# Choosing experts for four images at a time, and splitting the query and key products from a held score buffer, in a two-layer transformer kernel

## The chip, the cores and the metric

The kernel runs on one core of a Trainium2 chip. The metric is the device time of one execution, in microseconds. Before the change it is 2116.31 us, the median of 3 runs (2114.59 to 2121.39).

## What is computed

32 images of 256 tokens, 128 features, go through two layers. Each layer is an attention with 16 heads of 8 features and a feed-forward part in which a gate chooses among 8 experts (two in layer 0, one in layer 1). Cut to what matters:

```
for layer 0 and 1:
    h = layernorm(x) * (1 + ca) + sa
    q, k, v = h @ Wq, h @ Wk, h @ Wv            # layer 0 with biases, layer 1 after one more norm
    probs = softmax(q k^T * scale [+ bias])     # 16 heads, 256 x 256
    x = x + ga * attention(probs, v)
    h = layernorm(x) * (1 + cb) + sb
    logits = h @ Wgate                          # 8 experts
    x = x + gb * sum over chosen experts of weight * expert(h)
```

## The kernel before, in words

Four stages follow one another: attention of layer 0, experts of layer 0, attention of layer 1, experts of layer 1. A barrier lies between them. The change is in the two attention stages.

**Ticks.** `run_ticks` calls `tick` once for each value of i from -LEAD to B+LAG-1. In a tick every engine works through a list written out by hand, on several images at once: `at(off)` is image i+off. The order on each engine is fixed, and an engine waits on a semaphore where an input isn't there yet. `at(0)` is the image whose raw scores are computed for the row maxima (TensorE `scores_a` into the two A buffers, VectorE `row_max`, 16 heads), `at(-1)` the image whose scores are computed again with the maxima subtracted (`scores_b`, eight chunks of two heads into the two B buffers, exponentials by ScalarE in `exps`), weighted into values (`weigh`), and so on.

**Query and key products.** For image `at(1)`, TensorE writes q and k (128 x 256 each) into M0, a PSUM bank that a dozen small products share by turns (`m0_read` is the wait for whoever read it last). ScalarE copies them out with scale and bias (`read_qk`, L701 and L703 in layer 0, L698 and L699 in layer 1). GpSimd splits each float32 value into three bfloat16 parts with four operations (`split_qk`, L602 to L605). SyncE then issues twelve DMAs (`stack_up`) that lay the parts out in `stack`, from which the scores of the next tick are computed.

**Choosing experts.** After the gate product, VectorE copies the logits (`read_logits`). For every second image, `choose_first` (and in layer 0 `choose_second`) finds the chosen experts of both images at once, `count` on TensorE turns the choices into positions, and a tick later `weigh_choices` and `place` make the row numbers (`slot_in`). GpSimd then writes the rows of each image to DRAM by indirect DMAs (`scatter`, L640: four in layer 0, two in layer 1), with one tick for each image. The rows wait in `h2` (layer 0) or `h3` (layer 1), which have HELD = 4 places.

**Order on the engines around the change.** In a tick VectorE does: maxima 0 to 5 with norms between them, `read_logits`, `residual` in layer 1 (L917), maximum 6, `choose_first` in layer 0, in layer 1 `second_stats` and `outer_norm` (L826), maximum 7, and so on to maximum 15. ScalarE does: exponential of chunk 0, small copies, chunk 1, `read_qk`, chunk 2, `max_rows`, chunk 3, `values`, and chunks 4 to 7 with copies between. TensorE does: passes a0, a1, chunk 0, a2, `weigh`, `turn_h2`, a3, chunk 1, `project_qk`, a4, `turn_heads`, a5, `gate`, chunk 2, a6, `turn_max`, `weigh`, a7, chunk 3, `project_v`, a8, and so on to a15, `turn_max`, chunk 7 and a transpose. GpSimd does: split, in layer 1 `gate_values` (L619), `modulate`, `scatter`, in layer 1 `add_experts`.

Of the kernel before, what the change touches and what calls it, by code (L numbers as in the profile page):

```python
# [12 lines left out]
P = 128  # L13
B, S, D = 32, 256, 128
NT = S // P
GROUP = 2
GT = GROUP * NT
HELD = 4
# [6 lines left out]
TOK = 256  # L25
# [108 lines left out]
def build(nc, a, out):  # L134
    with ExitStack() as ctx:
# [6 lines left out]
        def dram(name, shape, dt=F32):  # L142
# [13 lines left out]
        ident_b = sb("ident_b", [P, P], BF16)  # L156
        slope_ident = sb("slope_ident", [P, HH, P], BF16)
# [40 lines left out]
        qk = sb("qk", [P, 2, S])  # L198
# [24 lines left out]
        h3 = sb("h3", [P, HELD, NT, WX])  # L223
# [21 lines left out]
        row_dest = [sb(f"row_dest{v}", [P, NT], I32) for v in range(HELD)]  # L245
        w1s = [sb(f"w1s{u}", [P, F]) for u in range(2)]
        w2s = [sb(f"w2s{u}", [P, FC, D]) for u in range(2)]
# [3 lines left out]
        hid = [sb(f"hid{u}", [P, FC, TOK]) for u in range(2)]  # L251
        yt = [sb(f"yt{v}", [P, NT, D]) for v in range(HELD)]

        Y = [hid[0][:, 2 * u:2 * u + 2, :].rearrange("p c (t d) -> p c t d", t=NT) for u in range(2)]
# [12 lines left out]
            (ident[:, :], a["ident"]), (ident_b[:, :], a["ident_b"].bitcast(BF16)), (slope_ident[:, :, :], a["slope_ident"].bitcast(BF16)),  # L267
# [17 lines left out]
        with nc.Block() as block:  # L285
# [40 lines left out]
            def _(dve):  # L326
# [16 lines left out]
                ch.mark(dve.tensor_copy(run[:, :], region_row[:, :]))  # L343
                ch.mark(dve.tensor_tensor(qs_bias[:, :], qk_bias[:, 0:1], q_scale[:, 0:1], ALU.mult))
# [39 lines left out]
LEAD, LAG = 3, 5  # L384
# [15 lines left out]
def group_done(at, off):  # L400

    return at(off) and at(off)[2] == GROUP - 1


def attention(nc, l, g):

    (X, XR, X1, st, mv, rs, xn, hT, qk, rem, parts, stack, vals, mx, mneg, mrow, probs, heads, rsum, On, OnT, yT,
     st2, mv2, rs2, xn2, front_rows, back_rows, xb, qs_bias, h2, h3, h2T, eps_col, lg, rt, r1, sel, slot_in, token_ids, run) = (g[n] for n in (
        "X XR X1 st mv rs xn hT qk rem parts stack vals mx mneg mrow probs heads rsum On OnT yT "
# [39 lines left out]
    def scattered_before(eng, q, v):  # L449
# [5 lines left out]
    stats, xn_ready, qk_f32, x1_ready, stats2, xn2_ready, logits_read, slots_ready, pos_read = signals(  # L455
        "stats", "xn_ready", "qk_f32", "x1_ready", "stats2", "xn2_ready", "logits_read", "slots_ready", "pos_read")
# [9 lines left out]
    split, h2_ready = signals("split", "h2_ready")  # L466
# [11 lines left out]
    with nc.Block() as block:  # L478
# [111 lines left out]
        def _(pool):  # L590
# [3 lines left out]
            def split_qk(b, k, u):  # L594

                pool.wait_ge(qk_f32.handle, qk_f32.after(b))

                for half in range(2):
                    pool.wait_ge(stack_in[u][half], stack_in.of(k - 1))
                p = parts[u]  # L600
                one = ones_col[:, :, :].broadcast_to([P, 2, S])
# [30 lines left out]
            def scatter(b, k, u, q, v):  # L632
                pool.wait_ge(slots_ready.handle, slots_ready.after(k))
# [3 lines left out]
                for c in range(n_choice):  # L637
                    for t in range(NT):
                        place = slot_in[v // GROUP][:, c, u * NT + t:u * NT + t + 1]
                        pool.indirect_dma_start(gathered[l], bass.IndirectOffsetOnAxis(ap=place, axis=0),  # L640
                                                (h3 if l else h2)[:, v, t, :], None).then_inc(scat_out[v], 16)

            def tick(at):
                if at(1):
                    split_qk(*at(1))
# [4 lines left out]
                if at(-5):  # L650
                    scatter(*held(at, -5))
# [1028 lines left out]
```

## Time and profile before

| | value |
|---|---|
| median of 3 runs | 2116.31 us |
| profiled execution, its own time | 2124.9 us |
| its span, first to last instruction | 2123.1 us |
| busy share of the span | TensorE 76%, VectorE 73%, ScalarE 47%, GpSimd 41% |
| mean granted TensorE clock | 0.936 of full speed |
| attention of layer 0, about | 46 to 810 us |
| experts of layer 0, about | 814 to 1109 us |
| attention of layer 1, about | 1114 to 1908 us |
| experts of layer 1, about | 1917 to 2123 us |

The shares are averages over four stages with different limits, so the table says where to look and not what bounds. A wait is given as "[time <- engine and line]": the idle time of the engine before that row and what ended it. Busy matrix products overlap in the profile, so the busy time of TensorE can't be added up from single rows.

### The profile page before, as it was taken

What the parts mean: (1) busy time and instruction counts of PE and PEld (TensorE: products, weight loads), DVE (VectorE), ACT (ScalarE), POOL (GpSimd) and SP (SyncE); (2) the same over time, 40 slices, a digit from 0 to 9 for tenths busy, and PEclk for the clock granted to TensorE, in tenths of its full rate; (3) what the DMA queues carried; (4) which work ended last, traced back from release to release, by engine and by line L of the source; (5) the groups of instructions that cost most, each with busy time, mean ns of one, the idle gap of its engine ahead of it and who ended that gap; (6) DMA issues with size and microseconds to landing.
All of it is one profiled execution on the core that took longest, in us unless ns stands there. A gap on an engine that the chain in (4) does not pass through costs nothing. (4 is left out here: it accounts for less than half of the span.)

```text
span 2123.1 us, 43990 instructions
## 1 busy us (share of the span) xinstructions
PE 1614.7 (76%) x14050; PEld 1145.8 (54%) x14050; DVE 1540.6 (73%) x4940; ACT 1002.2 (47%) x1846; POOL 878.5 (41%) x932
## 2 busy tenths in 40 slices
PE   2388888888888863999981777777777777753996
PEld 1256555555656542999971444444444444433886
DVE  4378878888888743777753879889888988853664
ACT  0166566666665541222221455565565565541543
POOL 0123353544444432555552335454445454430544
PEclk9899999999999986999995899999999999986998
DMA  4333343343333313222226544554455554525543
GB/s 112 75 67 65 78 74 79 75 79 74 79 74 77 68 39 77 72 72 74 72 58 165 96 87 103 113 110 105 110 110 103 114 111 104 98 63 163 134 124 82
DMA packets 267468, 193.11 MB, mean 91 GB/s; under 512 B 26095, under 2 KB 257297, under 8 KB 266468
## 3 DMA queue, kind: packets, MB, share of 16 engines
q1 hardware_dynamic: 251880, 155.28, 34.7%
q0 software_dynamic: 15360, 35.03, 5.4%
q8 instruction: 114, 1.87, 0.4%
q14 instruction: 114, 0.93, 0.2%
HBM read 95.21 MB, written 53.18 MB: 70 GB/s over the span
## 5 line engine op out<-in xcount | busy, mean ns | idle before, releaser
L871 DVE TENSOR_REDUCE mx<-A 128x2 f32<-128x512 f32 x1024 | 685.6, 681 | 196.2 <-PE A L1131 170.3
L725 ACT ACTIVATE probs<-B 128x1024 f32<-128x1024 f32 x512 | 523.2, 1022 | 370.1 <-PE B L1151 188.8
L1131 PE MATMUL A<-stack 126*128 126x256 bf16 x2048 | 393.5, 281 | 139.5 <-DVE mx L871 110.9
L1151 PE MATMUL B<-stack 128*128 128x256 bf16 x2048 | 360.2, 278 | 64.6 <-DMA stack<-mrow 64.6
L1131 PEld LDWEIGHTS A<-stack 126*128 126x128 bf16 x2048 | 163.0, 99 | 302.3 <-DVE mx L871 205.6
L1169 PE MATMUL M<-probs,vals 128*32 128x256 f32 x4096 | 287.2, 397 | 27.5 <-DVE On L894 24.7
L1151 PEld LDWEIGHTS B<-stack 128*128 128x128 bf16 x2048 | 196.8, 101 | 122.4 <-DMA stack<-mrow 87.5
L626 POOL TENSOR_TENSOR h<-xn,back_rows 128x256 f32<-128x256 f32 x64 | 46.3, 724 | 496.6 <-DVE xn L826 496.6
L640 POOL DMA_INDIRECT gathered<-h,slot_in x192 | 187.1, 974 | 100.7 <-DVE slot_in L1017 52.1
L1580 PE MATMUL A<-w2s,hid 128*128 128x128 f32 x1792 | 219.6, 276 | 8.4 <-issue 8.4
L1580 PEld LDWEIGHTS A<-w2s,hid 128*128 128x128 f32 x1792 | 208.8, 192 | 12.8 <-issue 12.8
L1384 POOL DMA_INDIRECT expert_out<-yt,row_dest x144 | 142.4, 989 | 156.9 <-DVE yt L1487 122.5
L1571 PE MATMUL B<-xtT,w1s 128*128 128x256 f32 x896 | 206.3, 385 | 0.0
L1154 PE MATMUL B<-dist,slope_ident 128*128 128x128 bf16 x1024 | 183.9, 220 | 0.0
L1169 PEld LDWEIGHTS M<-probs,vals 128*32 128x32 f32 x4096 | 122.2, 112 | 111.9 <-issue 44.0
L1571 PEld LDWEIGHTS B<-xtT,w1s 128*128 128x128 f32 x896 | 169.1, 194 | 21.0
L1529 ACT ACTIVATE hid<-B 128x1024 f32<-128x1024 f32 x72 | 73.7, 1024 | 212.4 <-PE B L1571 212.4
L602 POOL TENSOR_TENSOR parts<-qk,ones_col 128x512 bf16<-128x512 f32 x64 | 66.5, 1040 | 231.8 <-ACT qk L703 142.2
L1381 POOL DMA_INDIRECT out<-yt,row_dest x80 | 78.9, 987 | 127.5 <-DVE yt L1484 109.0
L671 ACT ACTIVATE rs<-mv,eps_col 128x2 f32<-128x2 f32 x192 | 56.0, 292 | 125.8 <-DVE mv L812 72.4
L1429 DVE TENSOR_SCALAR w1s<-w 128x512 f32 x112 | 54.9, 490 | 76.4 <-PE B L1571 69.3
L1562 PE MATMUL M<-ident,xt 128*128 128x128 f32 x224 | 44.0, 279 | 81.4 <-DMA xt<-gathered 81.4
(181 smaller groups left out, 2510.9 us busy)
## 6 DMA issues: line engine op xcount, KB each, us to landing
stack<-parts SPq DMA_DIRECT2D x768, 64.0 KB
xt<-gathered SPq DMA_DIRECT2D x112, 132.0 KB, 2.2
probs<-gathered SPq DMA_DIRECT2D x40, 256.0 KB, 3.2
w<-in_w SPq DMA_DIRECT2D x4, 2048.0 KB, 10.0
back_rows<-mod_rows SPq DMA_DIRECT2D x64, 128.0 KB, 3.7
x_mid<-X SPq DMA_DIRECT2D x64, 128.0 KB, 2.4
hid<-expert_out SPq DMA_DIRECT2D x64, 128.0 KB
X<-in_x SPq DMA_DIRECT2D x32, 128.0 KB, 3.7
```

What stands on the lines that cost most here:

```text
L640: pool.indirect_dma_start(gathered[l], bass.IndirectOffsetOnAxis(ap=place, axis=0), (h3 if l else h2)[:, v, t, :], None).then_inc(scat_out ...
L725: act.activation(probs[c % 4][:, :, :, :], Bp[c % 2][:, :, :, :], ACT.Exp, scale=EXP_SCALE[l][c // 4]).then_inc(b_exp.handle, 1)
L871: dve.tensor_reduce(mx[u][:, h, :], A[h % 2][:, :, :], AX.X, ALU.max).then_inc(a_max.handle, 1)
L1131: ins = pe.matmul(A[h % 2][:, t, :], stack[u][0:n, h, 0, t * P:(t + 1) * P], stack[u][0:n, h, 1, :], start=True, stop=True)
L1151: ins = pe.matmul(Bp[c % 2][:, j, t, :], stack[u][:, h, 1, t * P:(t + 1) * P], stack[u][:, h, 0, :], start=True, stop=(l == 1))
L1154: ins = pe.matmul(Bp[c % 2][:, j, t, t * P:(t + 1) * P], slope_ident[:, h % HH, :], dist[:, :], start=False, stop=True)
L1169: ins = pe.matmul(M1[VW * j:VW * j + VW, 0:S], vals[u][:, t, first:first + VW], probs[(2 * g + j // 2) % 4][:, j % 2, t, :], start=(q == 0 ...
L1381: ins = pool.indirect_dma_start(expert_out[l], dest, yt[s % HELD][:, t, :], None, bounds_check=B * S - 1, oob_is_err=False)
L1384: ins = pool.indirect_dma_start(expert_out[l], dest, yt[s % HELD][:, t, :], None)
L1529: act.activation(hid[u][:, :, :], src, ACT.Relu).then_inc(hidden.handle, 1)
L1571: ins = pe.matmul(dst[:, f, :], w1s[u][:, f * P:(f + 1) * P], xtT[u][:, :], start=True, stop=True)
L1580: ins = pe.matmul(A[u][:, t, 0:D], hid[u][:, f, t * P:(t + 1) * P], w2s[u][:, f, :], start=(f == 0), stop=(f == FC - 1))
```

## The change

- GROUP goes from 2 to 4: experts are chosen, counted and placed once for four images, on tiles twice as wide. HELD goes from 4 to 8, and the scatter of an image comes two ticks later (`at(-7)` for `at(-5)`), so LAG goes from 5 to 7. To make room, h3 shares its memory with buffers of the expert stages, which keep four output places (OUT = 4).
- The scale of q is multiplied into wq once, in the setup, by a row loaded with one more DMA.
- `project_qk` writes into the first half of B0 and no more into M0. ScalarE makes the high part straight from there (`high_part`), VectorE subtracts it from the products (`remainder`, after maximum 6), ScalarE casts the remainder (`mid_part`, between `max_rows` and chunk 3), GpSimd makes the low part (`low_part`, which is L605 of before). B0 is held from the product to the remainder, so that chunks 1, 2 and 3 of the scores all go into B1; the eight chunks use B0, B1, B1, B1, B0, B1, B0, B1 (before: by turns).

```diff
-GROUP = 2
+GROUP = 4
-HELD = 4
+HELD = 8
+OUT = 4
...
+                ch.mark(dve.tensor_tensor(wq[:, :, :], wq[:, :, :], scale_row[:, :, :], ALU.mult))
...
-LEAD, LAG = 3, 5
+LEAD, LAG = 3, 7
+BUFFER = (0, 1, 1, 1, 0, 1, 0, 1)
+HOLD = 4
...
-                ch.link(pool.tensor_tensor(p[:, :, 0, :], qk[:, :, :], one, ALU.mult))
-                ch.link(pool.tensor_tensor(rem[:, :, :], qk[:, :, :], p[:, :, 0, :], ALU.subtract))
-                ch.link(pool.tensor_tensor(p[:, :, 1, :], rem[:, :, :], one, ALU.mult))
-                pool.tensor_tensor(p[:, :, 2, :], rem[:, :, :], p[:, :, 1, :], ALU.subtract).then_inc(split.handle, 1)
+            def low_part(b, k, u):
+                pool.wait_ge(qk_mid.handle, qk_mid.after(b))
+                pool.tensor_tensor(parts[u][:, :, 2, :], rem[:, :, :], parts[u][:, :, 1, :], ALU.subtract)\
+                    .then_inc(split.handle, 1)
...
-                if at(-5):
-                    scatter(*held(at, -5))
+                if at(-7):
+                    scatter(*held(at, -7))
...
+            def high_part(b, k, u):
                 act.wait_ge(qk_proj.handle, qk_proj.after(b))
...
+                src, dst = Bp[0][:, 0, :, :], parts[u][:, :, 0, :]
                 if l:
+                    ins = act.activation(dst, src, ACT.Copy)
                 else:
+                    ch.mark(act.activation(dst[:, 0, :], src[:, 0, :], ACT.Identity, bias=qs_bias[:, 0:1]))
+                    ins = act.activation(dst[:, 1, :], src[:, 1, :], ACT.Identity, bias=qk_bias[:, 1:2])
+                ins.then_inc(qk_high.handle, 1)
+
+            def mid_part(b, k, u):
+                act.wait_ge(qk_rem.handle, qk_rem.after(b))
+                act.activation(parts[u][:, :, 1, :], rem[:, :, :], ACT.Copy).then_inc(qk_mid.handle, 1)
...
+            def remainder(b, k, u):
+                dve.wait_ge(qk_high.handle, qk_high.after(b))
+                dve.wait_ge(split.handle, split.after(b - 1))
+                src, high = Bp[0][:, 0, :, :], parts[u][:, :, 0, :]
+                if l:
+                    ins = dve.tensor_tensor(rem[:, :, :], src, high, ALU.subtract)
+                else:
+                    ch.mark(dve.scalar_tensor_tensor(out=rem[:, 0, :], in0=src[:, 0, :], scalar=qs_bias[:, 0:1],
+                                                     in1=high[:, 0, :], op0=ALU.add, op1=ALU.subtract))
+                    ins = dve.scalar_tensor_tensor(out=rem[:, 1, :], in0=src[:, 1, :], scalar=qk_bias[:, 1:2],
+                                                   in1=high[:, 1, :], op0=ALU.add, op1=ALU.subtract)
+                ins.then_inc(qk_rem.handle, 1)
...
             def project_qk(b, k, u):
                 pe.wait_ge(h_ready.handle, h_ready.after(b))
-                pe.matmul(M0[:, 0:S], wq[:, l, :], hT[u][:, :], start=True, stop=True)
-                pe.matmul(M0[:, S:2 * S], wk[:, l, :], hT[u][:, :], start=True, stop=True).then_inc(qk_proj.handle, 1)
+                pe.wait_ge(qk_rem.handle, qk_rem.after(b - 1))
+                pe.wait_ge(b_exp.handle, b_exp.after(b - 2, 1))
+                pe.matmul(Bp[0][:, 0, 0, :], wq[:, l, :], hT[u][:, :], start=True, stop=True)
+                pe.matmul(Bp[0][:, 0, 1, :], wk[:, l, :], hT[u][:, :], start=True, stop=True).then_inc(qk_proj.handle, 1)
...
-                pe.wait_ge(b_exp.handle, b_exp.after(b, c - 1) if c >= 2 else b_exp.after(b - 1, HH + c - 1))
+                if c == HOLD:
+                    if hold is None:
+                        pe.wait_ge(b_exp.handle, b_exp.after(b, 1))
+                    else:
+                        pe.wait_ge(qk_rem.handle, qk_rem.after(hold))
+                else:
+                    last = [d for d in range(c) if BUFFER[d] == BUFFER[c]]
+                    pe.wait_ge(b_exp.handle, b_exp.after(b, last[-1] + 1) if last else b_exp.after(b - 1, HH + c - 1))
...
                 if at(1):
-                    m0_read((h2T_read, -3))
                     project_qk(*at(1))
...
                 if at(-3):
-                    m0_read((qk_f32, 1))
                     gate(*at(-3))
```

## Rows read from the trace of the kernel before

**Rows 1.** Windows: busy us (instructions) of PE, PEld, DVE, ACT, POOL; clock, DMA, GB/s.
```profile
230.00:700.00 470.00, 408.68 (x4225) 278.74 (x4226) 387.46 (x1097) 286.05 (x515) 214.49 (x220) 1.00 0.38 76
1275.00:1840.00 565.00, 435.20 (x3859) 254.82 (x3858) 497.54 (x1556) 328.88 (x637) 265.60 (x297) 0.96 0.50 108
```

**Rows 2.** Source lines L701, L698: ns min/median/max, first and last start.
```profile
L701 ACT ACTIVATE qk<-M,qs_bias,q_scale x32: 557/563/564, 64.8 to 722.0; 128x256 f32<-128x256 f32 x32
...
L698 ACT ACTIVATE qk<-M,q_scale x32: 467/473/475, 1144.7 to 1839.8; 128x256 f32<-128x256 f32 x32
```

**Rows 3.** Timeline of TensorE, layer 0: start us, us, what, [idle before].
```profile
427.53 0.44 PE L1101 MATMUL M<-ident,On 128*128 128x128 f32 x2 [0.67 <-ACT vals L711]
...
438.91 0.28 PE L1151 MATMUL B<-stack 128*128 128x256 bf16 x1 [1.02 <-DMA stack<-mrow]
...
446.89 0.27 PE L1151 MATMUL B<-stack 128*128 128x256 bf16 x1
```

**Rows 4.** Waits, 230 to 700 us: us in total, times, longest us.
```profile
PE M L1187 <- ACT qk L703: 8.9, 21, 0.6
```

**Rows 5.** Timeline of ScalarE, layer 0, chunks 1 to 3.
```profile
442.25 1.02 ACT L725 ACTIVATE probs<-B 128x1024 f32<-128x1024 f32 x1
...
445.48 1.02 ACT L725 ACTIVATE probs<-B 128x1024 f32<-128x1024 f32 x1 [1.38 <-PE B L1154]
446.40 0.36 ACT L718 ACTIVATE mrow<-M 16x256 bf16<-16x256 bf16 x1
447.75 1.02 ACT L725 ACTIVATE probs<-B 128x1024 f32<-128x1024 f32 x1 [1.00 <-PE B L1154]
```

**Rows 6.** VectorE groups, 1275 to 1840 us: busy us, mean ns, idle before.
```profile
L917 DVE TENSOR_TENSOR h<-On,xb 128x256 f32<-128x256 f32 x25 | 30.6, 1224 | 1.3
L826 DVE TENSOR_SCALAR xn<-X,mv,rs 128x128 f32<-128x128 f32 x50 | 29.7, 633 | 0.0
...
L826 DVE TENSOR_SCALAR xn<-h,mv,rs 128x128 f32<-128x128 f32 x50 | 15.0, 343 | 0.0
...
L907 DVE TENSOR_TENSOR xb<-XR,M 128x256 f32<-128x256 f32 x25 | 10.5, 421 | 0.9
```

**Rows 7.** Timeline of GpSimd, layer 1: first and last of the split's four.
```profile
1453.07 1.04 POOL L602 TENSOR_TENSOR parts<-qk,ones_col 128x512 bf16<-128x512 f32 x1 [3.70 <-ACT qk L699]
...
1456.61 1.16 POOL L605 TENSOR_TENSOR parts<-rem,parts 128x512 bf16<-128x512 f32 x1
```

**Rows 8.** Timeline of VectorE, layer 1: placing, choosing, and L917 at the end.
```profile
1466.68 0.19 DVE L1007 TENSOR_TENSOR rt<-M,run 128x32 f32<-128x32 f32 x1
...
1467.42 0.17 DVE L1017 CAST slot_in<-r 128x4 int32<-128x4 f32 x1
...
1482.83 0.16 DVE L972 TENSOR_SCALAR h<-token_ids 128x4 f32<-128x4 f32 x1
...
1484.58 0.18 DVE L979 TENSOR_TENSOR rt<-lg,r 128x32 f32<-128x32 f32 x1
...
1877.39 0.43 DVE L917 TENSOR_TENSOR h<-On,xb 128x256 f32<-128x256 f32 x1
```

**Rows 9.** Timeline of TensorE, layer 1: the transpose of the maxima.
```profile
1467.12 0.28 PE L1138 MATMUL M<-ident_b,mneg 128*16 128x128 bf16 x2 [0.63 <-DVE run L1009]
```

**Rows 10.** Timelines of VectorE and GpSimd, the ends of both attention stages.
```profile
795.18 0.36 DVE L1017 CAST slot_in<-r 128x8 int32<-128x8 f32 x1
...
808.50 0.95 POOL L640 DMA_INDIRECT gathered<-h,slot_in  x1 [0.30 <-issue]
...
1903.19 0.96 POOL L640 DMA_INDIRECT gathered<-h,slot_in  x1 [1.41 <-DVE slot_in L1017]
...
1906.98 0.96 POOL L640 DMA_INDIRECT gathered<-h,slot_in  x1 [0.30 <-issue]
```

**Rows 11.** Timeline of VectorE in the setup.
```profile
12.66 2.65 DVE L340 MEMSET h<- 128x3104 f32 x1 [0.59 <-issue]
...
16.41 0.17 DVE L343 COPY run<-region_row 128x8 f32<-128x8 f32 x1 [1.07 <-DMA wmod<-in_wmod]
```

More of the change, by code:

```diff
@@ L244, in build @@
         row_weight = [sb(f"row_weight{u}", [P, 2, NT]) for u in range(2)]
[L245 to L247 removed]
+        row_dest = [sb(f"row_dest{v}", [P, NT], I32) for v in range(OUT)]
+        w1s = [shared[:, u * F:u * F + F] for u in range(2)]
+        w2s = [shared[:, (2 + u) * F:(3 + u) * F].rearrange("p (c d) -> p c d", c=FC) for u in range(2)]
         row_end = [sb(f"row_end{u}", [P, NT, W - D]) for u in range(2)]
@@ L465, in attention @@
                                         signal("pv", 4), signal("o_T", 2))
-    split, h2_ready = signals("split", "h2_ready")
+    h2_ready, = signals("h2_ready")
+    qk_high, qk_rem, qk_mid, split = signals("qk_high", "qk_rem", "qk_mid", "split")
     if l == 1:
@@ L632, in scatter @@
             def scatter(b, k, u, q, v):
-                pool.wait_ge(slots_ready.handle, slots_ready.after(k))
+                pool.wait_ge(slots_ready.handle, slots_ready.after(b // GROUP))
                 if l:
@@ L644, in tick @@
                 if at(1):
-                    split_qk(*at(1))
+                    low_part(*at(1))
                 if l and at(1):
@@ L750, in weights @@
             def weights(b, k, u):
-                act.wait_ge(w_den.handle, w_den.after(k))
+                act.wait_ge(w_den.handle, w_den.after(b // GROUP))
                 if l:
@@ L774, in tick @@
                 chunk(1)
-                step(read_qk, 1)
+                step(high_part, 1)
                 chunk(2)
@@ L778, in tick @@
                 step(max_rows, -1, 1)
+                step(mid_part, 1)
                 chunk(3)
@@ L991, in weigh_choices @@
                 row = group_rows(v)
-                dve.wait_ge(w_exp.handle, w_exp.after(k))
+                dve.wait_ge(w_exp.handle, w_exp.after(b // GROUP))
                 if l:
@@ L1003, in place @@
             def place(b, k, u, q, v):
-                dve.wait_ge(pos.handle, pos.after(k))
+                dve.wait_ge(pos.handle, pos.after(b // GROUP))
                 ch.settle()
@@ L1061, in tick @@
                 maxima(6, 1)
+                step(remainder, 1)
                 group(0, choose_first, -3)
@@ L1218, in chunk @@
                     if at(-1):
-                        scores_b(*at(-1), c)
+                        scores_b(*at(-1), c, at(1)[0] if at(1) else None)
                 def heads_step(step, off, g):
@@ L1312, in experts @@
     xt_in = Transfers([sem(f"xt_in{u}") for u in range(2)], 1)
-    yt_out = Transfers([sem(f"yt_out{v}") for v in range(HELD)], NT, 0)
+    yt_out = Transfers([sem(f"yt_out{v}") for v in range(OUT)], NT, 0)
     extra_in = Transfers([sem(f"extra_in{u}") for u in range(2)], 1)
@@ L1389, in _ @@
                     scatter(*tile(k, n))
-            for s in range(slots - HELD, slots):
-                pool.wait_ge(yt_out[s % HELD], yt_out.of(s // HELD))
+            for s in range(slots - OUT, slots):
+                pool.wait_ge(yt_out[s % OUT], yt_out.of(s // OUT))
         @block.vector
@@ L1652, in inputs_of @@
         "qk_bias": np.stack([bqkv[0:D][stacked], bqkv[D:2 * D][stacked]], 1),
-        "q_scale": np.stack([np.where(np.arange(D) < 64, HD ** -0.5, (2.0 / HD) ** 0.5), np.full(D, D ** -0.5)], 1).astype(f),
+        "q_scale": q_scale, "scale_row": np.broadcast_to(q_scale.T[None], (P, 2, P)).copy(),
         "vo_bias": np.stack([bqkv[2 * D:][out_rows], n["L0_attn_b_out"]], 1),
```

93 lines of the change are left out of this document (42 added, 51 removed).

## The prediction, made before the changed kernel was seen

> **What bounds the kernel now.** I read the page first, for the stages, and then the windows of the steady part of each attention stage [rows 1]. In layer 0 TensorE is busy for 408.68 of 470 us (87%) and VectorE for 82%; in layer 1 it is the other way round, VectorE 497.54 of 565 us (88%), TensorE 77%. So layer 0 is near TensorE's limit and layer 1 near VectorE's, and one edit has two prices. The source lines of the copies of q, one for each image, give the length of a tick [rows 2]: (722.0 - 64.8) / 31 = 21.2 us in layer 0, (1839.8 - 1144.7) / 31 = 22.4 us in layer 1. The sum below is so much per tick times about 30, plus what happens once.
>
> The timeline of TensorE in layer 0 shows what it waits for [rows 3]: 0.67 us before a transpose for the values, 1.02 us before chunk 0 for the row of maxima to land. The list of waits adds the gate's product, which waits for q and k to be copied out of M0 [rows 4]: 8.9 / 21 = 0.42 us in a tick. In layer 1 VectorE hardly pauses before its own work (the idle column is 0.0 to 1.3 us for 25 to 50 instructions [rows 6]); it is TensorE that waits for VectorE there.
>
> **The change, part by part.**
>
> *The gate's wait, layer 0.* q and k leave M0, so these 0.42 us go. They are kept only if what follows comes earlier too. The products of a chunk start 447.75 - 446.89 = 0.86 us before its exponential [rows 3, 5]. So chunk 2's products start at 445.48 - 0.86 = 444.6, or 444.2 after the change, and B1 is free when the exponential of chunk 1 ends, 442.25 + 1.02 = 443.3: 0.9 us of slack. Chunk 3's products start at 446.89 and B1 is free at 445.48 + 1.02 = 446.5: 0.4 us of slack, and both move together. The cast `mid_part` has to fit between the exponentials of chunks 2 and 3: 447.75 - 446.50 = 1.25 us, less 0.36 us for the copy of the maxima [rows 5]. A copy of 512 elements is not in the trace; from the 1.02 us for 1024 it is between half of that, 0.51, and three quarters, 0.77. I take 0.6 us, which leaves 0.3 us, if the remainder is there. So I take 0.4 us per tick: 30 x 0.4 = 12 us. Lower end: the exponentials slip by as much, 0. Upper end: TensorE idles 61 us in 22 ticks, 2.8 us per tick [rows 1]; less 0.67, 1.02 and 0.42 some 0.7 us remain, which I put down to VectorE; half as much choosing may give back half of it, so 0.75 us per tick, 22 us.
>
> *L917 in layer 1.* It takes 1224 ns on average [rows 6], but 0.43 us at the end of the stage, where no q and k are split any more [rows 8]. In the steady part it lies under GpSimd's four operations of the split, which last 1457.77 - 1453.07 = 4.7 us [rows 7]. After the change only the fourth is left, and it can't start before the remainder, which VectorE itself does after L917. So L917 loses 0.8 us per tick whatever else moves. The Trainium skill (SBUF — State Buffer, "Who interferes with whom") says that a VectorE instruction with two inputs in SBUF contends with a GpSimd instruction that reads SBUF. By that rule the remainder, which has one input in PSUM, waits for nobody and the sum is as below; were it held as L917 is, the sum would be 0.8 us per tick, 23 us, worse.
>
> *The remainder.* It is new on VectorE. L907 is the nearest row, one input in PSUM, 256 elements, 421 ns [rows 6]. With L1007, 32 elements from PSUM in 0.19 us [rows 8], the slope is (421 - 190) / 224 = 1.03 ns per element, so 512 elements take 421 + 264 = 0.69 us in one instruction (layer 1) and 0.84 us in two (layer 0). In layer 1 this is on the path. In layer 0 TensorE is the bound and choosing is rarer, so I take nothing; if the cover is gone it costs 0.84 us in a tick, which is inside the lower end above for every second tick. Bounds in layer 1: 0.6 to 0.84 us.
>
> *`outer_norm` in layer 1* (L826, xn from X). Each of its two instructions takes 633 ns against 343 ns for the same work from h [rows 6]: 0.58 us per tick lost beside L605 and what follows it on GpSimd. These stay, and by the order on VectorE `outer_norm` comes just after remainder and maximum 7, when the cast is over and `low_part` runs. I take no change; if the stall is gone it is 0.58 x 29 = 17 us more.
>
> *Choosing for four, layer 1.* Choosing takes 1484.76 - 1482.83 = 1.93 us less some 0.6 us of a maximum between, 1.3 us; placing 1467.59 - 1466.68 = 0.9 us [rows 8], and the two small instructions for the weight 0.3 us at the same size. That is 2.5 us for two images, 1.25 us per tick. Twice the width adds 32 elements, 33 ns by the slope above, to each of 15 instructions: 3.0 us for four images, 0.75 us per tick. The gain is 0.5 us per tick. Placing also holds up the transpose of the maxima by 0.63 us [rows 9], now in every fourth tick and not in every second: 0.16 us per tick. In layer 0 the choosing lies beside TensorE, the bound: nothing beyond the above.
>
> *The gate's wait, layer 1.* Between 0 and layer 0's 0.42 us [rows 4]; TensorE is late there for VectorE's sake only, so I take 0.15 us.
>
> *Layer 1, sum per tick:* -0.80 + 0.69 - 0.50 - 0.16 - 0.15 = -0.92 us, x 29 = -27 us.
>
> *The ends.* The last group is placed as soon as the last image is chosen, as before, but now four images wait for it and not two. In layer 0 the last `slot_in` was written at 795.2 and the last scatter began at 808.50 [rows 10]. Now all 16 scatters of four images follow. Their step is (1906.98 - 1903.19) / 3 = 1.26 us, so the last begins near 795.6 + 15 x 1.26 = 814.5: +6 us. In layer 1 eight follow where four did: 4 x 1.26 = +5 us. Nothing covers this, since the barrier comes after. Together +11 us.
>
> *The starts.* For the first image the path goes through the split: 4.7 us [rows 7]. Remainder, cast and `low_part` take 0.8 + 0.6 + 1.16 us and some 0.1 us between: 2.7 us. That is -2 us in each layer, -4 us.
>
> *The setup.* The memset of h3 doubles, so it is over 2.65 us later, after 17.9 us, where the loads were awaited until 16.41 [rows 11]. With the scaling of wq (256 elements, 0.4 us): +2 us. The added DMA lies under it.
>
> *Other edits.* The expert stages have the same instructions on other addresses: nothing. The two added ticks hold only scatters, counted above. SyncE's DMAs of the parts start when `low_part` ends, about when L605 ended before: cast over at 447.4, then 1.16 us, against a tick that begins ten microseconds later.
>
> **Sum:** -12 - 27 + 11 - 4 + 2 = -30 us. Against the profiled execution, 2124.9 us with 2123.1 us of span, that is 2095. The median of the runs lies 8.6 us under that execution, so I give 2116.3 - 30 = 2086 us.
>
> **Rivals.**
>
> *A. The held buffer becomes the wait (slower).* With chunks 1, 2 and 3 through one buffer, TensorE and ScalarE have to take turns: product, exponential, product. It decides once the exponential of chunk 2 ends over 0.4 us later, against TensorE, than in rows 5. If high part, remainder and cast come so late that chunks 2 and 3 slip by 1.2 us per tick, the cost is (1.2 - 0.4) x 61 = 49 us against the -30: 2135 us. For it: the cast waits in ScalarE's ordered queue for a VectorE instruction behind maximum 6, and every later exponential is queued behind the cast. Against it: ScalarE sits idle for 1.38 and 1.00 us before these two exponentials [rows 5].
>
> *B. The steady gains are small.* VectorE's relief in layer 1 is eaten at the edge of the tick by the landing of the maxima (1.02 us, which no edit touches), and the gate's wait in layer 0 turns into a longer one for the values (0.67 us now) [rows 3]. Then 0.3 us per tick in layer 1 (-9), 0.1 in layer 0 (-3), and +9 once: 2113 us. For it: the row of the landing. Against it: VectorE's 88% in layer 1, with 0.8 us of it that surely go.
>
> *C. More stalls go than I count.* `outer_norm` is freed as well (-17 us), and layer 0 reaches its upper end (-10 us): 2059 us. It hangs on some tenths of a microsecond in the start of `low_part`, which no row shows. The Trainium skill (same page and section) says that whoever of VectorE and GpSimd starts first keeps the port for the whole instruction; no row here shows who will be first.
>
> **How the numbers follow.** A measurement of this kernel can tell about 0.3% (6 us) from no change. The forecast (2072 to 2102 us) gets 0.58, C 0.16, B 0.16, A 0.10. The time is the likeliest, 2086 us. The range leaves out A and the far half of C: 2062 to 2110 us. Faster by over 0.3%: 0.58 + 0.16 and a third of B, 0.80. Within 0.3%: half of B and a little of A, 0.11. Slower: 0.09.
>
> **What would show each step.** The gate's row in layer 0 without a wait for ScalarE, and a tick there of 20.8 us. In layer 1 L917 near 430 ns, a remainder of about 690 ns, and a tick near 21.5 us. `outer_norm` still near 630 ns; if it falls to 340, C. Sixteen and eight scatters after the last `slot_in`, and 11 us for them in all. The prediction is wrong if TensorE shows a new wait for exponentials before chunks 2 and 3 (A), or if the ticks of layer 1 stay above 22 us (B).

## The result, and the profile after

The changed kernel takes 2126.03 us (median of 10 runs, 2114.45 to 2132.24) where the kernel before took 2117.52 us beside it (10 runs): a ratio of 1.0033, 95% interval 1.0018 to 1.0049. It is slower by a third of a per cent, where I forecast 1.4% faster. Its profiled execution took 2125.89 us, 2124.1 us of it span.

First the source lines that give the ticks: starts of the copies of q and k in layer 0 (L701) and layer 1 (L699).

```profile
L701 ACT ACTIVATE parts<-B,qs_bias x32: 472/473/475, 67.4 to 710.2; 128x256 bf16<-128x256 f32 x32
```
```profile
L699 ACT ACTIVATE parts<-B x32: 591/591/598, 1140.4 to 1833.1; 128x512 bf16<-128x512 f32 x32
```

With [rows 2] they cut both executions into five stretches. I add the two halves of the change, run by themselves (below).

| us | to the first copy of q | 31 ticks, layer 0 | between the layers | 31 ticks, layer 1 | rest | span |
|---|---|---|---|---|---|---|
| before | 64.8 | 657.2 | 422.7 | 695.1 | 283.3 | 2123.1 |
| after | 67.4 | 642.8 | 430.2 | 692.7 | 291.0 | 2124.1 |
| forecast, difference | +2 | -14 | +6 | -29 | +5 | -30 |
| measured, difference | +2.6 | -14.4 | +7.5 | -2.4 | +7.7 | +1.0 |

(The splitting of q and k follows their copy, so the forecast's -2 us for each first image stand in the columns of the two layers.) Layer 0 did what was forecast. Layer 1 gave 2 us of 29, and even that flatters it: the profiled execution of before holds two ticks of 26.2 and 27.8 us in layer 1, together some 8 us above the other ticks of their kind, and lies 7 us above the median of its runs. By the medians the kernel after is 8.5 us slower, and the spans differ by 1.0. In the windows it is still VectorE that is busiest there, 487.31 us of 565 where it was 497.54 [rows 1], and the stretch is hardly shorter:

```profile
230.00:700.00 470.00, 410.09 (x4303) 284.75 (x4300) 386.25 (x1021) 305.38 (x542) 144.65 (x155) 1.00 0.41 78
1275.00:1840.00 565.00, 423.62 (x3834) 259.12 (x3838) 487.31 (x1474) 329.30 (x627) 179.50 (x218) 0.95 0.51 106
```

VectorE's groups of layer 1, answering to [rows 6]: the remainder, the addition that was L917, and `outer_norm`.

```profile
L830 DVE TENSOR_SCALAR xn<-X,mv,rs 128x128 f32<-128x128 f32 x48 | 37.3, 816 | 0.0
L876 DVE TENSOR_TENSOR rem<-B,parts 128x512 f32<-128x512 f32 x25 | 17.0, 682 | 0.0
...
L934 DVE TENSOR_TENSOR shared<-On,xb 128x256 f32<-128x256 f32 x25 | 10.7, 426 | 1.2
```

426 ns (was 1224) and 682 ns are as forecast; 816 ns (was 633) is not.

Now four ticks of layer 1 in a row, from copy to copy. Columns: window in us, its length, busy time of TensorE, its weight loads, VectorE, ScalarE, GpSimd, then granted clock, DMA share, GB/s. The first tick chooses, the second places, the other two do neither (I call them free).

```profile
1464.95:1488.44 23.49, 18.50 (x155) 10.90 (x153) 20.84 (x64) 13.32 (x27) 7.45 (x9) 0.85 0.45 100
1488.44:1510.32 21.88, 16.30 (x164) 10.29 (x162) 20.05 (x63) 13.45 (x27) 7.44 (x9) 1.00 0.55 115
1510.32:1533.38 23.06, 17.50 (x155) 10.41 (x154) 18.91 (x56) 13.08 (x26) 7.44 (x9) 0.93 0.51 111
1533.38:1557.45 24.07, 17.39 (x155) 10.40 (x154) 18.91 (x56) 13.06 (x26) 7.42 (x9) 0.93 0.53 102
```

This is the heart of the case. A free tick has 1.1 us less of VectorE's work than a tick that places, and here takes 1.2 to 2.2 us more. Over 1285 to 1812 us the six ticks that place last 21.73 us on average, the six that choose 23.58, the eleven free ones 23.18. Choosing for four makes every second tick a free one. And in eight of the eleven free ticks the granted clock is below 1.00: part of the tick was at TensorE's lower level, 1.2 GHz, and the rest at 2.4 GHz.

What is different in a free tick is how the maxima's row reaches TensorE. Timelines of SyncE's queue, GpSimd and TensorE at the end of a tick that places, then of a free one (issue of the last load, of the scatters and of the row; chunk 0):

```profile
1409.56 0.57 SPq L508 DMA_DIRECT2D gb_row<-mod_rows  x1
1412.32 0.67 SPq L542 DMA_DIRECT2D stack<-mrow  x1
```
```profile
1412.99 1.01 POOL L640 DMA_INDIRECT gathered<-shared,slot_in  x1 [3.53 <-DVE slot_in L1034]
```
```profile
1414.55 0.28 PE L1179 MATMUL B<-stack 128*128 128x256 bf16 x1 [0.85 <-DMA stack<-mrow]
```
```profile
1431.14 0.43 SPq L508 DMA_DIRECT2D gb_row<-mod_rows  x1
1433.81 0.67 SPq L542 DMA_DIRECT2D stack<-mrow  x1
```
```profile
1431.44 1.01 POOL L640 DMA_INDIRECT gathered<-shared,slot_in  x1 [0.15 <-issue]
1432.76 0.96 POOL L640 DMA_INDIRECT gathered<-shared,slot_in  x1 [0.30 <-issue]
```
```profile
1437.30 0.28 PE L1179 MATMUL B<-stack 128*128 128x256 bf16 x1 [2.59 <-DMA stack<-mrow]
```

From issue to chunk 0 it is 2.2 us in the first and 3.5 us in the second. In the first the scatters wait for `slot_in` and start behind the row; in the second they start 2.4 and 1.0 us ahead of it, and the DMA engines are full when the row is sent (share of the 16 engines and GB/s at the end of each line):

```profile
1432.00:1433.00 1.00, 1.00 (x14) 0.34 (x7) 0.93 (x6) 0.01 (x1) 0.69 (x2) 1.00 0.66 141
1433.00:1434.00 1.00, 0.65 (x5) 0.35 (x4) 1.00 (x4) 0.97 (x4) 0.72 (x1) 1.00 1.08 305
1434.00:1435.00 1.00, 0.71 (x6) 0.39 (x5) 0.93 (x6) 1.00 (x2) 0.00 (x0) 1.00 1.17 349
1435.00:1436.00 1.00, 0.00 (x0) 0.00 (x0) 1.00 (x2) 0.14 (x1) 0.00 (x0) 1.00 0.99 339
1436.00:1437.00 1.00, 0.00 (x0) 0.00 (x0) 0.07 (x1) 0.00 (x0) 0.72 (x1) 1.00 0.60 154
```

TensorE stands still through the last two of these windows. That ticks that choose keep their 2.0 us from issue to chunk 0 fits: there choosing sends the row some 2 us later, behind the burst. The Trainium skill (DMA: Bandwidth & Descriptors, "Queues, rings and completion order") says that the descriptors which SyncE issues are consumed in order on each DMA engine. From that I infer that a small row waits behind the loads issued before it; the rows above agree, without proving it. The scatters come through another queue, GpSimd's.

The kernel before shows the same once. In its tick of 27.8 us, one that chooses, the row went out as close behind two scatters as in a free tick of the kernel after:

```profile
1488.23 1.01 POOL L640 DMA_INDIRECT gathered<-h,slot_in  x1 [0.15 <-issue]
1489.55 0.96 POOL L640 DMA_INDIRECT gathered<-h,slot_in  x1 [0.30 <-issue]
```
```profile
1490.59 0.67 SPq L534 DMA_DIRECT2D stack<-mrow  x1
```

Chunk 0 started 5.57 us after that, and the clock fell. In the 24 ticks around it the row took 2.0 to 2.3 us.

The landing and the clock can be told apart. In the three free ticks at full clock the length of the tick, less the time from the row's issue to chunk 0, is 19.2 to 19.3 us. In seven of the eight at a lower granted clock it is 20.6 to 21.8 us, so there the fall of the clock cost 1.3 to 2.6 us. In the eighth (1351.67 to 1373.26 us, clock 0.92) it is 19.2: there the clock was low some 6 us ahead of the row's issue, and cost nothing that can be seen.

### The profile page after: what moved, and what is told of

Same layout as the page of the kernel before. It is cut to its first block and busy times, and to the rows that moved or that the text cites. A ratio compares the mean times of both kernels' runs of the same rounds, so it can differ in the third digit from the quotient of the medians.

```text
span 2124.1 us, 43464 instructions
## 1 busy us (share of the span) xinstructions
PE 1593.6 (75%) x14034; PEld 1150.5 (54%) x14034; DVE 1525.7 (72%) x4725; ACT 1024.0 (48%) x1862; POOL 667.9 (31%) x740
## 5 line engine op out<-in xcount | busy, mean ns | idle before, releaser
L1152 PEld LDWEIGHTS A<-stack 126*128 126x128 bf16 x2048 | 168.5, 100 | 291.2 <-DVE mx L888 198.7
L1606 PE MATMUL A<-shared 128*128 128x128 f32 x1792 | 219.5, 276 | 9.1 <-issue 9.1
L604 POOL TENSOR_TENSOR parts<-rem,parts 128x512 bf16<-128x512 f32 x64 | 74.0, 1157 | 467.1 <-ACT parts L707 467.1
L1606 PEld LDWEIGHTS A<-shared 128*128 128x128 f32 x1792 | 208.8, 192 | 13.5 <-issue 13.4
L1597 PE MATMUL B<-xtT,shared 128*128 128x256 f32 x896 | 205.3, 383 | 0.0
L1597 PEld LDWEIGHTS B<-xtT,shared 128*128 128x128 f32 x896 | 168.0, 193 | 21.0
L1555 ACT ACTIVATE shared<-B 128x1024 f32<-128x1024 f32 x72 | 73.8, 1025 | 211.7 <-PE B L1597 211.7
L640 POOL DMA_INDIRECT gathered<-h,slot_in x128 | 124.1, 970 | 35.2 <-issue 34.4
L1455 DVE TENSOR_SCALAR shared<-w 128x512 f32 x112 | 55.2, 493 | 75.2 <-PE B L1597 68.3
```

The source lines that it names most:

```text
L604: pool.tensor_tensor(parts[u][:, :, 2, :], rem[:, :, :], parts[u][:, :, 1, :], ALU.subtract)\
L1152: ins = pe.matmul(A[h % 2][:, t, :], stack[u][0:n, h, 0, t * P:(t + 1) * P], stack[u][0:n, h, 1, :], start=True, stop=True)
L1597: ins = pe.matmul(dst[:, f, :], w1s[u][:, f * P:(f + 1) * P], xtT[u][:, :], start=True, stop=True)
L1606: ins = pe.matmul(A[u][:, t, 0:D], hid[u][:, f, t * P:(t + 1) * P], w2s[u][:, f, :], start=(f == 0), stop=(f == FC - 1))
```

## The experiments

Times are medians; the ratio is to the kernel before on the same chip, with its 95% interval. All kernels compute the whole reference.

| kernel | us | ratio |
|---|---|---|
| group_only | 2144.01 | 1.0116 (1.0090 to 1.0142) |
| split_only | 2101.88 | 0.9904 (0.9876 to 0.9931) |
| outer_first | 2182.05 | 1.0294 (1.0266 to 1.0323) |
| maxrow_first | 2129.54 | 1.0040 (1.0022 to 1.0058) |
| scatter_early | 2121.18 | 1.0003 (0.9987 to 1.0019) |
| loads_early | 2121.34 | 1.0003 (0.9986 to 1.0021) |
| both_early | 2110.96 | 0.9958 (0.9939 to 0.9976) |
| fill_16 | 2112.68 | 0.9967 (0.9955 to 0.9980) |
| split_fill | 2095.01 | 0.9872 (0.9856 to 0.9887) |
| split_fill_2 | 2090.75 | 0.9854 (0.9839 to 0.9869) |
| both_early_fill | 2105.53 | 0.9923 (0.9909 to 0.9936) |
| split_early_fill_2 | 2097.04 | 0.9880 (0.9865 to 0.9895) |

**The two halves.** `group_only` has the groups of four, the eight buffers, the shared memory and the later scatters, with the old way of q and k:

```diff
-GROUP = 2
+GROUP = 4
...
-HELD = 4
+HELD = 8
+OUT = 4
...
-LEAD, LAG = 3, 5
+LEAD, LAG = 3, 7
...
-                if at(-5):
-                    scatter(*held(at, -5))
+                if at(-7):
+                    scatter(*held(at, -7))
```

> Only the choosing for four images, the eight buffers and the shared memory; q and k are copied and split as before. Forecast's arithmetic: choosing and placing give 0.66 us per tick in layer 1 (-19 us), the ends cost 11 us as I forecast or 15 us as the trace after shows, the setup 2 us: about -4 us, 2112 us, with a tick of 21.8 us in layer 1. Theory now (what VectorE gains in layer 1 is lost at the tick's edge, where chunk 0 waits for the maxima): layer 1 gives at most a third of that, -6 us, the ends stay +15, so 2127 us and a tick above 22.2 us. L917 stays near 1220 ns under both, since GpSimd's split is back.

`split_only` is the changed kernel with `GROUP = 2`, `HELD = 4`, `LAG = 5` and the scatters again at `at(-5)`.

> Only the new way of q and k; experts are chosen for two images at a time. Forecast's arithmetic: layer 0 -12 us, layer 1 (-0.80 + 0.69 - 0.15) x 29 = -8 us, the first images -4 us: 2093 us. Theory now: layer 0 -14 us as measured, layer 1 a gain of 0.26 us per tick less 0.36 us for the slower outer_norm, so +3 us, first images -4 us, setup +0.5 us: about 2102 us, and the ends shorter than after the whole change by some 15 us. Rival (the split is what spoils layer 1: the clock falls, the maxima wait): a tick above 22.6 us in layer 1 and 2110 us or more.

One half gains 0.96% (about 20 us), the other loses 1.16% (about 25 us), and their product, 1.0019, is near the 1.0033 of both. `split_only` came out as expected (2102 us), `group_only` 17 us above the higher of its two forecasts (2127 us). Source lines of split_only and, below, of group_only:

```profile
L701 ACT ACTIVATE parts<-B,qs_bias x32: 467/472/475, 63.9 to 707.4; 128x256 bf16<-128x256 f32 x32
```
```profile
L699 ACT ACTIVATE parts<-B x32: 589/592/597, 1128.5 to 1813.7; 128x512 bf16<-128x512 f32 x32
```
```profile
L705 ACT ACTIVATE qk<-M,qs_bias,q_scale x32: 559/564/565, 67.0 to 719.1; 128x256 f32<-128x256 f32 x32
```
```profile
L702 ACT ACTIVATE qk<-M,q_scale x32: 469/475/476, 1150.2 to 1850.6; 128x256 f32<-128x256 f32 x32
```

| us, less before | to first copy | layer 0 | between | layer 1 | rest |
|---|---|---|---|---|---|
| split_only | -0.9 | -13.7 | -1.6 | -9.9 | +2.3 |
| group_only | +2.2 | -5.1 | +8.4 | +5.3 | +6.9 |

These are single executions, and before's slow ticks are in layer 1's column. The split's share is close to the sum that the forecast's terms give it (-12 - 0.26 x 29 - 4 + 0.5 = -23 us; -20 measured). Choosing for four, which those terms put at -6 us, costs 25: 15 at the ends (8.4 + 6.9), 2 in the setup, and layer 1 gets some 13 us longer once before's two slow ticks are allowed for; layer 0 gets 5 us shorter, which does not come on top of the split's 13.7 in the kernel after (14.4). Its ticks show the pattern with the old split too: a free tick of group_only has 18.75 us of VectorE's work, the tick that places two ticks earlier 19.94.

```profile
1505.72:1527.55 21.83, 16.94 (x163) 10.19 (x162) 19.94 (x62) 13.32 (x26) 10.77 (x12) 1.00 0.52 116
...
1550.69:1574.89 24.20, 17.99 (x154) 10.34 (x153) 18.75 (x55) 13.03 (x26) 10.74 (x12) 0.93 0.48 103
```

**outer_first** takes away the stall of `outer_norm`:

```diff
+                layer(1, outer_norm, 2)
                 step(remainder, 1)
                 group(0, choose_first, -3)
                 rows(1, second_stats, -2)
-                layer(1, outer_norm, 2)
```

> The whole change, with outer_norm of layer 1 moved ahead of the remainder on VectorE, so that neither low_part nor gate_values runs beside it. If GpSimd's instructions are what holds it, its two instructions fall from 816 ns to about 340 ns each. Theory (the edge of the tick eats VectorE's relief): the time falls by less than 0.3 us per tick, 2117 to 2126 us. Rival (VectorE's work is the bound of every tick of layer 1): (0.816 - 0.34) x 2 = 0.95 us per tick, 27 us, about 2098 us. Slower than the whole change (over 2130 us) if the later cast delays the exponential of chunk 3 and with it TensorE.

It was slower by more than either theory gave. Its group of `outer_norm`, its wait for the row over 1275 to 1840 us (it was 32.7 us in 25 waits in the kernel after), and one free tick:

```profile
L830 DVE TENSOR_SCALAR xn<-X,mv,rs 128x128 f32<-128x128 f32 x46 | 13.7, 341 | 0.0
```
```profile
PE B L1179 <- DMA stack<-mrow: 46.3, 24, 3.6
```
```profile
1463.23 0.67 SPq L542 DMA_DIRECT2D stack<-mrow  x1
```
```profile
1467.59 0.82 PE L1179 MATMUL B<-stack 128*128 128x256 bf16 x3 [3.45 <-DMA stack<-mrow]
```

`outer_norm` is freed as expected, 341 ns for 816. But counted from the copy of q, the parts leave 1.2 us later and the row of maxima, in most ticks, only 0.4 us later: from the start of `low_part` to the row's issue it is 10.15 us here, 10.97 in the free ticks after, 11.3 in ticks that place, 12.8 and more in those that choose. The row then takes 3.5 to 4.5 us (2.4 in the one free tick without scatters ahead of it), 2.3 to 3.5, 2.0 to 2.3 and 2.0 us. The less time SyncE's parts and loads have before the row is sent, the longer the row waits, though in ticks that place the scatters stand behind it too.

The row is not all of it. The free ticks of 1275 to 1840 us are 25.5 us long on average (up to 26.6) where they were 23.2. Of these 2.3 us the longer landing is 1.0 (3.8 us for 2.9). Some 0.5 on average is more time between the copy of q and the row's issue. The rest goes with the clock, which is granted at 0.81 to 0.93 in all eleven. The danger that I had named came as well: ScalarE waits longer for the remainder (it was 16.7 us in 25 waits), and in the free ticks at 1473 us and, for the kernel after, 1352 us the exponential of chunk 3 starts 5.5 us after the copy of q where it started 4.3 us after it. Whether the 0.5 us are its doing or that of VectorE's later maxima, no run tells.

```profile
ACT parts L707 <- DVE rem L876: 43.1, 23, 2.2
```

**maxrow_first** sends the row earlier:

```diff
+                step(max_rows, 0, 0)
                 layer(1, rms_rsqrt_of, -2)
-                step(max_rows, 0, 0)
```

> The whole change, with the copy of the maxima's row ahead of rms_rsqrt_of on ScalarE at the end of a tick in layer 1. It is about 0.45 us earlier in a tick without choosing. Theory (chunk 0's wait for the landing is what ends a tick of layer 1, and TensorE's clock falls when that wait is 1.6 us): at least 0.4 us per tick less, 2126 - 12 = 2114 us or below, with a wait of 1.2 us or less before chunk 0 and fewer ticks at a low granted clock. Rival (VectorE is the bound, and its rms_norm comes later): same or slower, 2126 to 2135 us, and VectorE waits for ScalarE before L964.

The same time as after, within what can be told, and so in the range of the rival. The row of a free tick went 0.43 us earlier against the scatters and took 2.6 to 3.9 us. My theory of that moment (the copy on ScalarE is late) fell: an earlier row is a longer wait.

**Moving the traffic.** `scatter_early`, in layer 1 (with `LAG` 8), and `loads_early`:

```diff
+                if l and at(-8):
+                    scatter(*held(at, -8))
                 if at(-2):
                     modulate(*held(at, -2))
-                if at(-7):
+                if l == 0 and at(-7):
                     scatter(*held(at, -7))
```
```diff
-                    sp.wait_ge(h_rows.handle, h_rows.after(b - 2))
+                    sp.wait_ge(h_stats.handle, h_stats.after(b - 2))
...
+                if l and at(3):
+                    load_front(*at(3))
                 if at(1):
                     stack_up(*at(1), 0)
...
-                if l and at(3):
-                    load_front(*at(3))
```

> The whole change, but in layer 1 a group's scatters are issued one tick later and ahead of modulate in GpSimd's order, so that they start some 12 us before the maxima's row is sent and not 2.4 and 1.0 us before it. Theory (the row of maxima lands late because the transfers issued just before it, scatters above all, are still on the DMA engines): in ticks without choosing or placing the row lands in about 2.0 us where it took 2.3 to 3.5, TensorE's clock stays at its higher level and such a tick takes 21.5 us where it took 23.5: 12 such ticks x 1.9 = -23 us, 2103 us. Rival (it is the loads of the image three ahead that stand before the row, or the clock falls for another reason): the landing stays at 2.3 us and more, 2120 to 2130 us.

> The whole change, but in layer 1 SyncE issues the loads of X, expert_out, front_rows and gb_row ahead of the parts of q and k, not between these and the maxima's row. Theory (what is issued before the row of maxima delays its landing): half as much stands before the row, so it lands in 2.0 to 2.5 us, and the time falls by 10 to 20 us, to 2106 to 2116 us. Rival (only the scatters matter): no change, 2120 to 2130 us. Second rival (the bytes are late wherever they stand, and the parts now land late): new waits of TensorE for the parts, and slower.

> Both moves at once, loads and scatters in layer 1. Theory (traffic before the maxima's row): the landing is 2.0 us in every tick and the ticks without choosing or placing fall to 21.5 us or below; 2095 to 2103 us. If the moves are of no use because DMA as a whole or VectorE is the bound, 2120 us or more.

Against the kernel after (by the ratios, 1.0003 and 0.9958 to 1.0033) each alone gives about 6 us, both together 16, so scatters and loads share the blame; each of these differences of 6 us is uncertain by some 5. All three fell short: the single moves ended where their rivals had them (2120 to 2130 us), and both together gained 16 us of the 23 to 31 expected. With both moved the row takes 2.0 to 2.3 us in free ticks, and these take 21.7 us on average (11 of them, 21.3 to 23.1). Ticks of both_early that choose, place, and two free ones:

```profile
1462.39:1485.87 23.48, 18.52 (x155) 10.91 (x153) 20.87 (x64) 13.31 (x26) 7.45 (x9) 0.85 0.48 104
1485.87:1507.61 21.74, 16.39 (x164) 10.19 (x163) 20.02 (x63) 13.52 (x27) 7.46 (x9) 1.00 0.52 115
1507.61:1528.99 21.38, 16.04 (x155) 9.93 (x154) 19.37 (x56) 13.08 (x26) 7.43 (x9) 1.00 0.46 117
1528.99:1550.57 21.58, 16.02 (x155) 9.95 (x153) 19.38 (x56) 13.08 (x27) 7.45 (x9) 1.00 0.52 114
```

**Keeping the clock up.** `fill_16` leaves the traffic as it is and gives TensorE something to do before chunk 0 (the results are overwritten):

```diff
+                if l == 1 and c == 0:
+                    pe.wait_ge(b_exp.handle, b_exp.after(b - 1, HH - 1))
+                    for _ in range(16):
+                        pe.matmul(Bp[0][:, 1, 0, 0:P], ident_b[:, :], dist[:, :], start=True, stop=True)
                 if c % 4 == 0:
                     pe.wait_ge(m_in[u][c // 4], m_in.of(k))
```

> The whole change, with sixteen small products (128 x 128, bf16, results overwritten) on TensorE in layer 1 while it waits for the maxima's row before chunk 0: about 0.9 us of work inside a wait of 0.6 to 2.6 us. Theory (the long wait lets TensorE's clock fall to its lower level, and that costs about 1.9 us in each such tick beside the wait itself): more ticks at a granted clock of 1.00, and 2106 to 2116 us. Rival (the low clock comes from elsewhere in the tick, or costs nothing because VectorE is the bound): granted clock as before in most ticks, and 2122 to 2132 us, since in ticks with a short wait the products cost up to 0.3 us each.

Extra work made the kernel 14 us faster (0.9967 to 1.0033). Ticks of fill_16 that choose, place, and two free ones:

```profile
1466.00:1489.88 23.88, 18.37 (x171) 11.21 (x169) 21.58 (x64) 13.31 (x26) 7.45 (x9) 0.93 0.48 101
1489.88:1511.57 21.69, 17.04 (x180) 11.21 (x179) 20.05 (x63) 13.46 (x27) 7.45 (x9) 1.00 0.50 113
1511.57:1533.46 21.89, 16.89 (x171) 10.97 (x169) 18.90 (x56) 13.08 (x27) 7.44 (x9) 1.00 0.54 116
1533.46:1555.45 21.99, 16.90 (x171) 11.00 (x169) 18.91 (x56) 13.08 (x27) 7.45 (x9) 1.00 0.55 114
```

The row still takes 2.2 to 3.5 us (2.67 on average, 2.87 in the kernel after, 2.11 in both_early), and yet eight of the eleven free ticks are at full clock now and their mean is 22.15 us, where it was 23.18 in the kernel after and 21.71 in both_early. The products so gave 1.03 us, 0.2 of it by a landing that happened to be shorter, and some 0.8 by the clock. Of the 1.5 us between the kernel after and both_early, about half is the longer landing and about half the clock that falls behind TensorE's standstill. At full clock the length less the landing is the 19.2 to 19.3 us of above in seven of these eight ticks (19.5 in one). The clock can be seen on one line, the sixteen products of the values, in the kernel after with the clock up and down:

```profile
1454.08 1.07 PE L1197 MATMUL M<-probs,vals 128*32 128x256 f32 x16 [0.60 <-DVE On L911]
```
```profile
1571.88 1.59 PE L1197 MATMUL M<-probs,vals 128*32 128x256 f32 x16 [0.60 <-DVE On L911]
```

The second is in a tick that chooses; it starts 2.3 us after the end of a wait of 1.64 us for a maximum (head 13's scores, at 1569.56). `split_fill_2` fills that wait too, with twenty products ahead of the scores of head 13.

> The new way of q and k with choosing for two images, and the sixteen small products before chunk 0 in layer 1. With two images there is no tick without choosing or placing, and the landing of the maxima took 2.0 us in nearly every tick of split_only. Theory (the products only help where the wait for the landing is long): little to gain here, 2095 to 2103 us beside split_only's 2102. Rival (they hold the clock up in the ticks with choosing as well): -15 us or more, 2087 us or less.

> As split_fill, and in the ticks of layer 1 that choose, twenty more small products on TensorE ahead of the scores of head 13, where it waits 1.5 us for VectorE and runs at the lower clock soon after. Theory (a tick that chooses takes 23.2 us and not 21.6 because the clock falls there, not because of VectorE's 1 us of work): these ticks fall to about 22 us, 12 to 14 of them x 1.2 = -15 us, 2085 us. Rival (VectorE's work makes the tick long): no change, 2095 to 2103 us.

Two ticks of split_only that choose and place, and two of split_fill_2 that place and choose:

```profile
1410.86:1434.00 23.14, 17.41 (x155) 10.57 (x153) 20.93 (x64) 13.31 (x27) 7.53 (x9) 0.93 0.51 107
1434.00:1455.63 21.63, 16.20 (x160) 10.17 (x158) 19.99 (x63) 13.43 (x27) 7.46 (x9) 1.00 0.51 115
```
```profile
1517.20:1538.76 21.56, 16.93 (x176) 11.08 (x174) 19.91 (x63) 13.45 (x28) 7.46 (x9) 1.00 0.55 115
1538.76:1561.29 22.53, 19.30 (x191) 13.57 (x189) 20.15 (x64) 13.11 (x26) 7.45 (x9) 0.92 0.53 109
```

The first set of products gives 7 us with groups of two, the second 4 more. A tick that chooses falls from 23.1 to 22.6 us on average, less than half of what I expected: about 0.5 us of its length was the clock. The kernel before bears this out: its three ticks at full clock that choose took 22.5 to 22.6 us. Five of the eleven in split_fill_2 still have a granted clock of 0.92 or 0.93, as the one above, and take 22.5 to 22.8 us all the same; so it matters where in a tick the clock is low, and I have no run on that. 0.9 us over a placing tick stays, with nearly the same amount of VectorE's work in both (20.15 and 19.91 us). I take it for the place of that work, in front of a maximum for which TensorE waits; this is argued and not shown. The last two runs combine the edits.

> Choosing for four, with loads and scatters of layer 1 moved early and the sixteen products before chunk 0. Theory: all three work on the same ticks (without choosing or placing), which both_early had already brought to 21.3 to 21.9 us in most cases; so 2103 to 2110 us. Rival (each acts by itself): 2111 - 13 = 2098 us.

> Choosing for two over eight buffers, loads and scatters of layer 1 early, and both sets of small products. With two images a scatter stands ahead of the row of maxima only in ticks that choose, where the row is sent late anyway. Theory: the moves add nothing to split_fill_2, and the larger memset costs 2 us: the same time as split_fill_2 or up to 3 us more. Rival: DMA traffic lengthens these ticks too, and it is 5 us or more faster.

With groups of four the three edits together reach 2105.5 us: less than the sum, since they repair the same ticks, and inside the range expected. In the profiled executions layer 1 (first to last copy) takes 672 us there, 682 in split_fill and 674 in split_fill_2: repaired, choosing for four gains some 9 us in layer 1 over split_fill, and that does not pay for the 15 us at the ends and 2 in the setup. With groups of two, moving the traffic on top costs 6 us instead of the 0 to 3 expected; 2.6 of it are before the first copy of q (67.4 us there, 64.8 in split_fill_2). The traces have the rest between the layers (+2.0 us) and in layer 1 (+4.6, in an execution 2.8 us above its median); I have no run on their cause. split_fill_2 is the fastest kernel of the study, 1.5% under the kernel before and 1.8% under the changed one, with groups of two.

## Why the prediction was wrong, point by point

- *The gate's wait, layer 0* (-12): right. It is gone from the waits; the last 25 ticks of layer 0 went from 21.46 to 21.03 us on average, 0.43 us for the 0.42 forecast. With its first ticks the layer gave 14.4 us, and 13.7 by the split alone. TensorE waits for the values as before, and 7.8 us in 22 waits for the logits to be read are new:

```profile
PE M L1119 <- ACT vals L714: 15.4, 23, 0.7
PE M L1159 <- DVE lg L980: 7.8, 22, 0.7
```

- *L917* (-0.80 us per tick) and *the remainder* (+0.69): right to 0.01 us. That the remainder wouldn't be held by GpSimd was not put to the test: none of the 32 has a GpSimd instruction beside it.
- *`outer_norm`* (no change): wrong by 2 x (816 - 633) = 0.37 us per tick. `low_part` began 0.37 us before it (1561.92 against 1562.29 us in one tick) and `gate_values` followed; outer_first shows that this overlap is the cause. The Trainium skill (SBUF — State Buffer, "Who interferes with whom") says that the one who issues first holds the shared port for the whole instruction. GpSimd started first, and the rows agree: each of VectorE's two instructions ends 0.08 us after the GpSimd instruction beside it (1357.35 and 1358.03 after 1357.27 and 1357.95 us). Rival C, that it would be freed, had the sign wrong.
- *Choosing for four, layer 1* (-0.50 and -0.16 us per tick, -19 in all): this step failed. Layer 1 of group_only is not shorter but longer: its tick, over all 31, is 22.6 us and not the 21.8 that this step gives. VectorE did save the time (18.91 us in a free tick for 20.05 and 20.84), and the tick got longer. The error stands in the step *Layer 1, sum per tick*: it added VectorE's savings as if VectorE set the length of each tick. With a full clock and a row that lands in about 2 us, a tick that doesn't choose takes 21.3 to 21.9 us, be it with 18.9, 19.4 or 20.0 us of VectorE's work in it (ticks that place in outer_first and both_early_fill took 22.2 to 22.6), so work taken from a tick already near 21.6 us gives nothing. What choosing less often can give is the 0.9 to 1.9 us by which a tick that chooses is longer, and the late row and the falling clock took that back.
- *Rival B* (0.16) named the place, the landing of the maxima at the tick's edge, but not the price: it took 1.02 us as fixed [rows 3] and 0.3 us per tick as kept. The wait grows to 2.6 us as the row is sent close behind the scatters and loads, and the clock falls behind it.
- *Rival A* (0.10) didn't come: no new wait of TensorE for exponentials before chunks 2 and 3.
- *The ends* (+11): the mechanism was right, the size 15 us. After the last `slot_in` of layer 0 the last scatter starts 802.42 - 781.11 = 21.3 us later, where it was 13.3 [rows 10]: +8.0, not +6. In layer 1 it is the forecast +5: eight scatters start from 1899.62 to 1908.48, where four did from 1903.19 to 1906.98 [rows 10]. Some 3 us more lie ahead of them: from the last copy of q to the first of these scatters it is 66.6 us, where it was 63.4. Why, I didn't trace.

```profile
781.11 0.17 DVE L1034 CAST slot_in<-r 128x16 int32<-128x16 f32 x1
```
```profile
802.42 0.96 POOL L640 DMA_INDIRECT gathered<-h,slot_in  x1 [0.30 <-issue]
```
```profile
1899.62 0.96 POOL L640 DMA_INDIRECT gathered<-shared,slot_in  x1 [4.76 <-DVE slot_in L1034]
...
1908.48 0.96 POOL L640 DMA_INDIRECT gathered<-shared,slot_in  x1 [0.30 <-issue]
```

- *Setup and first images* (+2 and -4): the setup's memset takes 5.23 us where it took 2.65 [rows 11], and the first copy of q is 2.6 us later; with groups of two it is 0.9 us earlier. The gain of the first images shows behind that copy: the first three ticks went from 58.3 to 55.1 us in layer 0 and from 59.8 to 58.7 in layer 1 (53.0 and 57.3 in split_only). That is -4.2 us, some 1 of it the steady gain of the ticks: the mechanism and about the size.

```profile
13.31 5.23 DVE L344 MEMSET shared<- 128x6208 f32 x1 [1.24 <-issue]
```

Open: what sets the 21.3 to 21.9 us of an undisturbed tick, in which neither TensorE (16.0 us) nor VectorE is full; and why the row took 2.3 us in some free ticks and 3.5 in others with the same issue times (2.31 us before chunk 0 at 1528.07, 3.43 before that at 1552.25 us); and what the clock costs by its place in the tick.

## What to carry to other kernels

Before savings on the busiest engine are added up per tick, compare ticks that have that work with ticks that don't: if their lengths don't differ, the engine isn't what a tick waits for. A small transfer on which the next stage waits should be issued ahead of the large ones or well behind them (here the move gave 16 us), and whoever lets it be sent sooner must look at what is still on the DMA engines. A wait of TensorE costs more than its own length when its clock falls behind it (here 1.3 to 2.6 us more); a few idle products can give back most of that.

## What the runs showed of the hardware that I had not expected

- The landing of an 8 KB row goes with what was issued before it: 2.0 us from issue to chunk 0 in ticks that choose, up to 4.5 us (outer_first; 5.6 once in the kernel before) behind some 1.6 MB issued in the 10 us before it (six parts of 64 KB, 832 KB of loads, 0.40 MB of scatters).
- Sixteen products of 128 x 128 in a wait of 0.6 to 2.6 us, in each tick of layer 1, made the kernel after 0.7% faster, with the granted clock at 1.00 in eight of eleven free ticks where it was in three.
- Two VectorE instructions of 341 ns each take 816 ns when one GpSimd instruction (1.16 us) starts 0.37 us before them and another follows it.
